# Two attention layers in one fused transformer kernel: row maxima split on VectorE and turned in 32x32 blocks instead of by TensorE

## The chip, the cores and the metric

The kernel runs on one NeuronCore of a Trainium2 chip. The metric is the device time of one launch, in microseconds (us). The engines are TensorE (PE; its weight loads are shown apart as PEld), VectorE (DVE), ScalarE (ACT), GpSimd (POOL) and SyncE (SP), which here issues most of the DMAs.

## The reference

Sixteen sequences of 256 tokens with 128 features pass through four blocks, each followed by a residual sum and a layer norm: a causal attention with 16 heads of 8 features (low-rank projections of queries and keys), a gated MLP 128-512-512-512-128, a second attention without a mask, and an expert MLP with top-1 routing.

```python
x = _layernorm(x + _L0_attn_ref(x, ...))   # causal, softmax(q k / sqrt(8)) v
x = _layernorm(x + _L0_ffn_ref(x, ...))    # silu gate, two 512x512 layers with gelu
x = _layernorm(x + _L1_attn_ref(x, ...))   # softmax(q k) / sqrt(128), then v
x = _layernorm(x + _L1_ffn_ref(x, ...))    # top-1 of 8 experts, each a rank-4 addition
```

## The kernel before, in words

The work is cut in 16 chunks, one sequence each, and four stages, `A0`, `F0`, `A1`, `F1` (attention, MLP, attention, expert MLP). Attention needs the scores twice. `pass1` computes them with queries on the partitions, from bf16 pieces of queries and keys (72 rows, `ROWS`), only to find the maximum of each query's row: VectorE reduces each PSUM bank into columns of `top`, [128 queries, 2 query blocks, head] (L799 for A1 and the first chunks of A0; for the other chunks of A0 a fused add and minimum, L788, since there the causal mask must be added). `pass2` computes the scores again with keys on the partitions. It must subtract the maximum of each query, and queries now run along the free dimension. So the negated maximum enters the product as three more rows of the queries' operand, bf16 pieces that add up to the fp32 value: 75 rows (`ROWSM`) at L1113. ACT takes the exponential (L643), and `values` (L1131) multiplies by v.

Getting the maxima from `top` into those three rows is the step `maxima`. It is done once per chunk and attention, except for chunk 0 of A0 (which adds the maxima in fp32 and stays as it is), and for the last chunk of A1 it is done in two halves (`early` for the first 8 heads). That makes 30 whole ones and 2 halves. Its parts before the change:

- PE waits until all maxima of the chunk are made, then transposes the two blocks of `top` with the identity into a shared PSUM bank (L1081; L1092 for the early half).
- DVE waits for that, and splits the 16x256 maxima from PSUM in three bf16 parts (cast, subtract, cast, subtract: L829, L831, L833, L835; L812 to L818 for the early half) into `tsplit`.
- SP waits for the parts and issues three DMAs of 8 KB, one for each row of `qrow` (L505; L513 for the early half).
- PE's `pass2` of this chunk waits for the DMAs (`trows`).

Each engine runs its steps in the order of a string, `SEQUENCE`, one letter for a step, written out for the whole kernel. The steps of several chunks are interleaved in it: while one chunk is in attention A0, an earlier one is in the MLP and a still earlier one in A1. An engine takes its letters strictly in turn, so a letter that waits holds all behind it. A second string, `BANK_TABLE`, gives each PE step its PSUM bank. The letters `warm` are multiplications of the identity (L988) with no use for the result.

## Time and profile before

| | |
|---|---|
| median of 3 runs | 895.47 us (893.18 to 896.65) |
| profiled execution, its own time | 896.33 us |
| its span in the trace | 894.6 us |
| PE busy | 867.6 us, 97% |
| PEld busy | 683.4 us, 76% |
| DVE busy | 700.9 us, 78% |
| ACT busy | 461.5 us, 52% |
| POOL busy | 195.8 us, 22% |
| TensorE's granted clock, mean | 0.984 |

The profiled execution has 1.7 us around its span and is 0.9 us above the median of the three runs. PE's busy time is a union of matmuls of which each is shown with its whole latency, so neighbours overlap, and 97% does not mean that PE works at its peak. The chain that ended last tells through which engine the end was reached.

### The profile page before, as it was taken

What the parts mean: (1) busy time and instruction counts of PE and PEld (TensorE: products, weight loads), DVE (VectorE), ACT (ScalarE), POOL (GpSimd) and SP (SyncE); (2) the same over time, 40 slices, a digit from 0 to 9 for tenths busy, and PEclk for the clock granted to TensorE, in tenths of its full rate; (3) what the DMA queues carried; (4) which work ended last, traced back from release to release, by engine and by line L of the source; (5) the groups of instructions that cost most, each with busy time, mean ns of one, the idle gap of its engine ahead of it and who ended that gap; (6) DMA issues with size and microseconds to landing.
All of it is one profiled execution on the core that took longest, in us unless ns stands there. A gap on an engine that the chain in (4) does not pass through costs nothing.

```text
span 894.6 us, 19356 instructions
## 1 busy us (share of the span) xinstructions
PE 867.6 (97%) x7132; PEld 683.4 (76%) x7132; DVE 700.9 (78%) x2490; ACT 461.5 (52%) x861; POOL 195.8 (22%) x395
## 2 busy tenths in 40 slices
PE   8989999999999999999999999999999999999997
PEld 6867687877667876688777887788866887878866
DVE  5667758778899769984998859996799859845874
ACT  2323454638456436665655736544466655582382
POOL 6332212003410133011500123012320314010211
PEclk9999799999899999999999999999999999999999
DMA  7324032321232034402142033210333022002200
GB/s 255 110 79 117 16 90 66 90 68 43 81 107 74 1 91 116 119 3 74 43 136 54 21 90 109 70 52 19 112 110 91 3 78 57 24 8 71 78 14 13
DMA packets 47982, 63.78 MB, mean 71 GB/s; under 512 B 5504, under 2 KB 41936, under 8 KB 43184
## 3 DMA queue, kind: packets, MB, share of 16 engines
q1 hardware_dynamic: 46208, 57.67, 22.7%
q10 hardware_dynamic: 1680, 4.87, 1.5%
q8 instruction: 57, 0.93, 0.4%
q14 instruction: 37, 0.30, 0.1%
HBM read 47.48 MB, written 14.29 MB: 69 GB/s over the span
## 4 chain that ended last, share of the span: by engine, by line
PE 74%; DVE 12%; DMA 5%; ACT 4%; issue 2%; SPq 2%; POOL 0%; ACTq 0%; POOLq 0%; DVEq 0%
PE banks L1182 23%; PE banks L1131 10%; PE banks L1113 8%; PE banks L1060 6%; PE banks L1164 6%; PE banks L1238 5%; DVE top L799 4%; DMA krow<-scratch 3%; PE banks L1001 2%; PE banks L1211 2%; PE banks L1051 1%; ACT prob L643 1%; PE banks L1143 1%; ACT L643 1%; PE banks L988 1%
## 5 line engine op out<-in xcount | busy, mean ns | idle before, releaser
L643 ACT ACTIVATE prob<-banks 128x384 f32<-128x384 f32 (+1 forms) x512 | 246.6, 552 | 102.8 <-PE banks L1113 57.6
L799 DVE TENSOR_REDUCE top<-banks 128x2 f32<-128x512 f32 (+1 forms) x268 | 166.9, 678 | 11.7 <-PE banks L1060 8.4
L1113 PE MATMUL banks<-qrow,krow 75*128 75x256 bf16 x992 | 148.7, 264 | 6.4 <-ACT prob L643 3.4
L788 DVE CUSTOM_DVE_ANT_0 banks<-banks,above 128x128 f32<-128x128 f32 x448 | 144.3, 386 | 11.8 <-PE banks L1060 7.6
L1060 PE MATMUL banks<-krow,qrow 72*128 72x256 bf16 x752 | 126.0, 276 | 3.7 <-ACT prob L643 1.9
L1131 PE MATMUL banks<-prob,v 128*32 128x256 f32 (+1 forms) x2048 | 121.2, 365 | 2.7 <-POOL prob L585 1.9
L1113 PEld LDWEIGHTS banks<-qrow,krow 75*128 75x128 bf16 x992 | 85.5, 99 | 43.7 <-ACT prob L643 13.6
L1182 PE MATMUL banks<-glu,wh 128*128 128x256 f32 x512 | 118.5, 385 | 0.2 <-DVE glu L900 0.2
L1182 PE MATMUL banks<-hid,wh 128*128 128x256 f32 x512 | 118.3, 385 | 0.0
L578 POOL TENSOR_TENSOR ln_rstd<-ln_var,minus_half 128x2 f32<-128x2 f32 x64 | 44.9, 705 | 300.1 <-DVE ln_var L879 299.7
L657 ACT ACTIVATE hid<-banks 128x512 f32<-128x512 f32 x64 | 38.1, 597 | 134.8 <-PE banks L1182 134.6
L1182 PEld LDWEIGHTS banks<-glu,wh 128*128 128x128 f32 x512 | 96.0, 192 | 13.9 <-DVE glu L900 0.6
L1182 PEld LDWEIGHTS banks<-hid,wh 128*128 128x128 f32 x512 | 96.1, 192 | 13.6 <-ACT prob L643 0.5
L1131 PEld LDWEIGHTS banks<-prob,v 128*32 128x32 f32 x2048 | 56.8, 111 | 50.0 <-issue 15.3
L1060 PEld LDWEIGHTS banks<-krow,qrow 72*128 72x128 bf16 x752 | 65.6, 99 | 27.5 <-ACT prob L643 5.7
L585 POOL TENSOR_SCALAR_AFFINE_SELECT prob<-prob 128x512 f32<-128x512 f32 x128 | 83.7, 654 | 0.0
L583 POOL TENSOR_TENSOR pool_carrier<-minus_half 128x1 f32<-128x1 f32 x128 | 28.4, 222 | 248.4 <-ACT prob L643 244.7
L573 POOL TENSOR_TENSOR resid<-x,rows 128x256 f32<-128x256 f32 x48 | 34.8, 726 | 143.9 <-DVE ln_sum L866 143.2
L1164 PE MATMUL banks<-xt,w 128*128 128x256 f32 x256 | 61.5, 387 | 0.3 <-ACT xt L648 0.2
L788 DVE DVE_READ_ACCUMULATOR2_ANT top<- 128x1 f32 x448 | 61.5, 137 | 0.0
L841 DVE STREAM_TRANSPOSE osum<-banks 128x256 f32<-128x256 f32 x64 | 28.2, 440 | 32.4 <-PE banks L1131 32.2
L1164 PEld LDWEIGHTS banks<-xt,w 128*128 128x128 f32 x256 | 46.9, 193 | 8.0 <-ACT xt L648 0.5
(125 smaller groups left out, 1181.2 us busy)
## 6 DMA issues: line engine op xcount, KB each, us to landing
qrow<-scratch SPq DMA_DIRECT2D x30, 576.0 KB
krow<-scratch SPq DMA_DIRECT2D x90, 192.0 KB
scratch<-split SPq DMA_DIRECT2D x93, 128.0 KB, 1.8
xt<-in_xt SPq DMA_DIRECT2D x16, 128.0 KB, 3.0
wh<-in_wh ACTq DMA_DIRECT2D x2, 1024.0 KB, 9.3
out<-xout SPq DMA_DIRECT2D x16, 128.0 KB, 2.2
x<-in_x SPq DMA_DIRECT2D x15, 128.0 KB, 3.6
qrow<-tsplit SPq DMA_DIRECT2D x90, 8.0 KB, 1.8
```

Of the source, the lines that this page charges most:

```text
L578: nc.gpsimd.tensor_tensor(ln_rstd[s][:], ln_var[s][:], minus_half[:], ALU.pow).then_inc(rstd[s], 1)
L585: nc.gpsimd.affine_select(out=diag, in_=diag, compare_op=ALU.is_ge, fill=0.0, base=0, pattern=[[0, 2], [0, QB], [1, P]], channel_multiplie ...
L643: nc.scalar.activation(prob[s][:, j % 2, g, 0:wide], banks[:, b, 0:wide], ACT.Exp, scale=1.0 / float(np.sqrt(np.float32(HD))) if s == A0 e ...
L657: nc.scalar.activation(hid[layer][:, 2 * m:2 * m + 2, :].rearrange("p m t -> p (m t)"), banks[:, g, :], ACT.Gelu).then_inc(gelued, 1)
L788: done = nc.vector.tensor_tensor_reduce(out=bank[:, g * wide:(g + 1) * wide], in0=bank[:, g * wide:(g + 1) * wide], in1=above[:, 2 * P - w ...
L799: nc.vector.tensor_reduce(out=dst, in_=src, axis=AX, op=ALU.max, negate=True).then_inc(maxed[s], 1)
L1060: done = nc.tensor.matmul(at, queries(h, qb), keys(h, 2), start=True, stop=not masked, skip_group_check=True)
L1113: done = nc.tensor.matmul(bank[:, kb * SEQ:(kb + 1) * SEQ - q0], krow[s][n % DEEP[s]][0:ROWSM, h, kb * P:(kb + 1) * P], qrow[s][n % DEEP[s ...
L1131: done = nc.tensor.matmul(banks[32 * i:32 * i + 32, g, q0:SEQ], v[s][:, kb, GROUP * j + i, :], prob[s][:, j % 2, i, kb * SEQ:(kb + 1) * SE ...
L1164: done = nc.tensor.matmul(banks[:, g, i * TOK:(i + 1) * TOK], w12[:, side, (2 * m + i) * P:(2 * m + i + 1) * P], xt[F0][n % AHEAD][:], sta ...
L1182: done = nc.tensor.matmul(banks[:, g, i * TOK:(i + 1) * TOK], wh[:, layer, k, (2 * m + i) * P:(2 * m + i + 1) * P], (glu, hid[0])[layer][: ...
L1238: done = nc.tensor.matmul(banks[:, g, t * D:(t + 1) * D], src[:, k, t * P:(t + 1) * P], w[:, k, :], start=k == 0, stop=k == HB - 1)
```

## The change

The maxima are no longer turned by PE. `top` shrinks to [128, 32], column 2h + q for head h and query block q. VectorE splits it in three bf16 parts as it lies, [128, 3, 32] (`tpart`), and then turns it with four transposes of 32 partitions by 3 x 32 elements, which land in `tsplit`, [32 (head, block), 3, 128]. SP's three DMAs per chunk now read 32 rows of 128 elements in place of 16 rows of 256, the same bytes. PE has no step for it, and no PSUM bank is used. The step is called `tops` (`half_tops` for the early half, which computes and turns all 32 columns, and of which SP takes 16 rows). Both fall on DVE and SP only. Chunk 0 of A0 keeps PE's transposes. Two memsets of `top` on POOL are gone.

```diff
-        top = {s: sb(f"top{s}", [P, QB, P]) for s in (A0, A1)}
-        tsplit = {s: sb(f"tsplit{s}", [32 + HALF, PARTS, SEQ], BF16) for s in (A0, A1)}
-        trest = {s: sb(f"trest{s}", [32 + HALF, SEQ]) for s in (A0, A1)}
+        top = {s: sb(f"top{s}", [P, HEADS * QB]) for s in (A0, A1)}
+        tpart = {s: sb(f"tpart{s}", [P, PARTS, HEADS * QB], BF16) for s in (A0, A1)}
+        tsplit = {s: sb(f"tsplit{s}", [32, PARTS, P], BF16) for s in (A0, A1)}
+        trest = {s: sb(f"trest{s}", [P, HEADS * QB]) for s in (A0, A1)}
...
+            def spread_tops(s, n, heads, there):
                 for i in range(PARTS):
+                    sp.dma_start(qrow[s][n % DEEP[s]][ROWS + i:ROWS + i + 1, heads, :].rearrange("o h (q t) -> o (h q) t", q=QB),
+                                 tsplit[s][heads.start * QB:heads.stop * QB, i, :]).then_inc(there, DMA)
...
-                    sp.dma_start(qrow[s][n % DEEP[s]][ROWS + i:ROWS + i + 1, there, :],
-                                 tsplit[s][0:HALF if n == HALVED[s] else HEADS, i, :]).then_inc(trows[s], DMA)
...
+            def parts_of_tops(s, done, k):
+                t, r = tpart[s], trest[s][:]
+                nc.vector.tensor_copy(t[:, 0, :], top[s][:]).then_inc(done, 1)
+                dve.wait_ge(done, k + 1)
+                nc.vector.tensor_tensor(r, top[s][:], t[:, 0, :], ALU.subtract).then_inc(done, 1)
+                dve.wait_ge(done, k + 2)
+                nc.vector.tensor_copy(t[:, 1, :], r).then_inc(done, 1)
+                dve.wait_ge(done, k + 3)
+                nc.vector.tensor_tensor(t[:, 2, :], r, t[:, 1, :], ALU.subtract).then_inc(done, 1)
+                dve.wait_ge(done, k + 4)
+                for b in range(P // 32):
+                    turned = nc.vector.transpose(tsplit[s][:, :, bass.ts(b, 32)], t[bass.ts(b, 32)])
+                turned.then_inc(done, 1)
+
+            def tops(s, n):
+                k = rowed_before(s, n)
+                dve.wait_ge(maxed[s], S1[s] * n + S1[s])
...
+                    dve.wait_ge(trows[s], NTOPS * k)
+                parts_of_tops(s, tparts[s], 5 * k)
...
             def maxima(s, n, g):
-                dve.wait_ge(top_full[s], 1 * n + 1)
...
-                nc.vector.tensor_copy(t[:, 0, :], src).then_inc(tparts[s], 1)
...
             def maxima(s, n, g):
-                pe.wait_ge(maxed[s], S1[s] * n + S1[s])
...
-                for qb in range(QB):
-                    done = nc.tensor.transpose(banks[:, g, qb * P:(qb + 1) * P], top[s][:, qb, :], ident[:])
-                done.then_inc(top_full[s], 1)
-                last.used(g, tparts[s], 4 * rowed_before(s, n) + 2)
```

The strings `SEQUENCE` of all five engines and `BANK_TABLE` are new. The number of every other kind of step is the same, the 34 `warm` steps among them; their order differs in many places by a few steps. Two places show the kind.

On PE, the end of the scores of chunk 3 of A0 (`maxima`), which is the third of the 32. L1060 is `pass1`, L1113 `pass2`, L1131 `values`, L1182 a layer of the MLP, L1238 its last layer. Before:

```order
L1060 MATMUL banks<-krow_1,qrow_1 128x256 x2
L1113 MATMUL banks<-qrow_0,krow_0 128x256
L1113 MATMUL banks<-qrow_0,krow_0 128x128
L1182 MATMUL banks<-hid,wh 128x256 x8
L1081 MATMUL banks<-ident,top 128x128 x2
L1131 MATMUL banks<-prob,v 32x256 x4
L1131 MATMUL banks<-prob,v 32x128 x4
L1131 MATMUL banks<-prob,v 32x256 x4
L1131 MATMUL banks<-prob,v 32x128 x4
L1238 MATMUL banks<-w,hid 128x128 x8
```

and with the change (L1059 is `pass1`, L1169 the layer, L1118 `values`, L1225 the last layer):

```order
L1059 MATMUL banks<-krow_1,qrow_1 128x256 x2
L1169 MATMUL banks<-hid,wh 128x256 x8
L1059 MATMUL banks<-krow_1,qrow_1 128x256 x2
L1118 MATMUL banks<-prob,v 32x256 x4
L1118 MATMUL banks<-prob,v 32x128 x4
L1118 MATMUL banks<-prob,v 32x256 x4
L1118 MATMUL banks<-prob,v 32x128 x4
L1225 MATMUL banks<-w,hid 128x128 x8
```

The transposes are gone, and the last step of `pass1` now stands behind the layer instead of ahead of it.

On DVE, the end of the last chunk of A1. L799 reduces a bank of scores, L866 to L879 are the sum and the statistics of a layer norm, and L829 to L835 split the last 8 heads' maxima. Before:

```order
L799 TENSOR_REDUCE top<-banks 128x2 x3
L866 TENSOR_TENSOR ln_sum<-banks,resid 128x256
L871 BN_STATS ln_parts<-ln_sum 128x6 x2
L874 MEMSET dve_carrier 128x1
L876 BN_AGGR ln_stat<-ln_parts 128x2 x2
L879 TENSOR_SCALAR ln_var<-ln_stat 128x2
L829 CAST tsplit<-banks 16x256
L831 TENSOR_TENSOR trest<-banks,tsplit 16x256
L833 CAST tsplit<-trest 16x256
L835 TENSOR_TENSOR tsplit<-trest,tsplit 16x256
```

and with the change (L794 reduces, L806 to L815 are the new step, L865 on is the layer norm):

```order
L794 TENSOR_REDUCE top<-banks 128x2 x3
L806 CAST tpart<-top 128x32
L808 TENSOR_TENSOR trest<-top,tpart 128x32
L810 CAST tpart<-trest 128x32
L812 TENSOR_TENSOR tpart<-trest,tpart 128x32
L815 STREAM_TRANSPOSE tsplit<-tpart 32x3x32 x4
L865 TENSOR_TENSOR ln_sum<-banks,resid 128x256
L870 BN_STATS ln_parts<-ln_sum 128x6 x2
L873 MEMSET dve_carrier 128x1
```

The step now follows the last reduction directly, where the layer norm's sum and statistics stood between.

## Rows read from the trace of the kernel before

**Rows 1.** Page, part 4: the chain that ended last, by engine.

```profile
PE 74%; DVE 12%; DMA 5%; ACT 4%; issue 2%; SPq 2%; POOL 0%; ACTq 0%; POOLq 0%; DVEq 0%
```

**Rows 2.** Windows of 50 us: PE, PEld, DVE, ACT, POOL busy (instructions), granted clock, DMA.

```profile
250.00:300.00 50.00, 48.11 (x410) 35.51 (x409) 47.56 (x204) 30.70 (x55) 4.95 (x8) 1.00 0.26 71
350.00:400.00 50.00, 49.72 (x427) 37.65 (x427) 47.12 (x200) 32.01 (x56) 2.92 (x6) 1.00 0.26 73
400.00:450.00 50.00, 49.09 (x408) 39.60 (x408) 34.58 (x105) 28.65 (x53) 17.86 (x38) 1.00 0.22 62
450.00:500.00 50.00, 48.35 (x380) 37.69 (x379) 45.16 (x167) 29.85 (x52) 4.17 (x6) 0.97 0.31 83
550.00:600.00 50.00, 49.81 (x456) 37.40 (x455) 47.20 (x187) 26.40 (x51) 6.50 (x10) 1.00 0.27 79
650.00:700.00 50.00, 48.84 (x454) 34.99 (x455) 48.20 (x184) 27.17 (x55) 5.50 (x11) 1.00 0.30 85
```

**Rows 3.** Groups by line and form: the first split step and the transposes.

```profile
L829 DVE CAST tsplit<-banks 16x256 bf16<-16x256 f32 x31 | 12.4, 401 | 16.0 <-PE banks L1081 15.8
L1081 PE MATMUL banks<-ident,top 128*128 128x128 f32 x62 | 12.4, 281 | 0.0
L1081 PEld LDWEIGHTS banks<-ident,top 128*128 128x128 f32 x62 | 7.4, 143 | 3.2 <-issue 1.4 <-DVE top L799 0.9
```

**Rows 4.** The chain in order of time: first and last of 22 pieces of L1081, and L1092.

```profile
55.60 0.45 PE banks L1081 x2
...
855.11 0.37 PE banks L1092 x2
...
860.56 0.27 PE banks L1081 x2
```

**Rows 5.** Timeline of DVE, 111 to 118 us, and of PE there.

```profile
113.91 0.41 DVE L829 CAST tsplit<-banks 16x256 bf16<-16x256 f32 x1 [4.78 <-PE banks L1081]
115.11 0.41 DVE L835 TENSOR_TENSOR tsplit<-trest,tsplit 16x256 bf16<-16x256 f32 x1
...
108.33 5.32 PE L1182 MATMUL banks<-hid,wh 128*128 128x256 f32 x16
113.49 0.38 PE L1081 MATMUL banks<-ident,top 128*128 128x128 f32 x2
```

**Rows 6.** Timeline of DVE, 218 to 223 us: small steps, overlapping writes, a transpose.

```profile
218.27 0.18 DVE L914 TENSOR_TENSOR pick<-logit,best 128x16 f32<-128x16 f32 x1
218.48 0.18 DVE L915 TENSOR_TENSOR pick<-pick,ranks 128x16 f32<-128x16 f32 x1
...
221.42 0.45 DVE L855 STREAM_TRANSPOSE yt<-osum 128x256 f32<-128x256 f32 x1
221.79 0.58 DVE L773 TENSOR_TENSOR v<-banks,rows 128x64 f32<-128x64 f32 x4
```

**Rows 7.** The chain in order of time, 221 to 231 us: wait for the rows.

```profile
224.52 0.56 SPq L505
...
225.12 0.59 SPq L505
...
225.75 3.81 DMA qrow<-tsplit
```

**Rows 8.** Timeline near the end, DVE: the last chunk's maxima.

```profile
858.38 1.95 DVE L799 TENSOR_REDUCE top<-banks 128x2 f32<-128x512 f32 x3 [0.16 <-PE banks L1060]
...
861.71 0.41 DVE L829 CAST tsplit<-banks 16x256 bf16<-16x256 f32 x1
```

**Rows 9.** Page, part 6: a row's DMA, KB each, median us to landing.

```profile
qrow<-tsplit SPq DMA_DIRECT2D x90, 8.0 KB, 1.8
```

**Rows 10.** Timeline: first and last of eleven L829 in the five busy windows of DVE.

```profile
265.42 0.41 DVE L829 CAST tsplit<-banks 16x256 bf16<-16x256 f32 x1
...
692.32 0.37 DVE L829 CAST tsplit<-banks 16x256 bf16<-16x256 f32 x1
```

**Rows 11.** A window of 10 us, columns as in the 50 us windows: the clock.

```profile
100.00:110.00 10.00, 9.94 (x70) 6.12 (x71) 5.75 (x35) 6.88 (x15) 6.18 (x16) 0.57 0.01 2
```

More of the change, by code:

```diff
@@ L140 @@
+        "zMlTzMGGTzMTzMGKGTTTTT"
     ),
@@ L184, in sequence @@
         n, i = divmod(seen[letter], len(parts_of(name, stage)))
-        if name == "early":
+        if name in ("early", "half_tops"):
             n = EARLY[stage]
         seen[letter] += 1
-        if stage == A0 and (name in ("qk", "fetch") or name == "maxima" and engine == "sp"):
+        if stage == A0 and name in ("qk", "fetch", "tops"):
             n += 1
@@ L432, in build @@
         S2 = HEADS
+        NTOPS = PARTS * DMA
         NWEIGHTS1 = 4 * DMA
@@ L536, in _ @@
             nc.gpsimd.memset(hid[1][:].rearrange("p m t -> p (m t)"), 0.0).then_inc(wex_cleared, 1)
-            nc.gpsimd.memset(top[A0][:].rearrange("p q h -> p (q h)"), 0.0)
             nc.gpsimd.memset(minus_half[:], -0.5)
@@ L779, in pass1 @@
                 bank = banks[:, b, :]
-                h, to = GROUP * j, top[s]
-                if n == HALVED[s]:
-                    h, to = (32 + h, top_early[s]) if j < HALVES else (h - HALF, top[s])
+                h, to = GROUP * j, top[s][:].rearrange("p (h q) -> p q h", q=QB)
+                if u == 0:
+                    if j == 0 and rowed_before(s, n) > 0:
+                        dve.wait_ge(tparts[s], 5 * rowed_before(s, n) - 3)
+                    elif j == HALVES and n == HALVED[s]:
+                        dve.wait_ge(early_parts[s], 2)
                 if s == A0 and n >= BY_PE:
@@ L924, in route @@
                 done.then_inc(routed, 1)
-            walk(dict(scale=scale, qk=split_, v=v_, pass1=pass1, maxima=maxima, early=early, osum=bring, outputs=outputs, project=project, down=sum_,
+            walk(dict(scale=scale, qk=split_, v=v_, pass1=pass1, maxima=maxima, tops=tops, half_tops=half_tops, early=early, osum=bring, outputs=outputs, project=project, down=sum_,
                       norm=norm, gated=gate, route=route), "dve")
@@ L1074, in maxima @@
             def maxima(s, n, g):
-                pe.wait_ge(maxed[s], S1[s] * n + S1[s])
+                pe.wait_ge(maxed[s], S1[s])
                 last.wait(pe, g)
-                if s == A0 and is_first(n):
-                    turn_tops(1, g).then_inc(top_full[s], 1)
-                    return
-                for qb in range(QB):
-                    done = nc.tensor.transpose(banks[:, g, qb * P:(qb + 1) * P], top[s][:, qb, :], ident[:])
-                done.then_inc(top_full[s], 1)
-                last.used(g, tparts[s], 4 * rowed_before(s, n) + 2)
+                turn_tops(1, g).then_inc(top_full, 1)
             def early(s, n, g):
-                pe.wait_ge(maxed[s], S1[s] * n + S1[s] // 2)
+                pe.wait_ge(maxed[s], S1[s] // 2)
                 last.wait(pe, g)
-                if s == A0:
-                    turn_tops(0, g).then_inc(early_full[s], 1)
-                    return
-                for qb in range(QB):
-                    done = nc.tensor.transpose(banks[:, g, qb * P:(qb + 1) * P], top_early[s][:, qb, :], ident[:])
-                done.then_inc(early_full[s], 1)
-                last.used(g, early_parts[s], 2)
+                turn_tops(0, g).then_inc(early_full, 1)
             def pass2(s, n, j, g, b):
                 if j == 0 and g == 0 and n == HALVED[s]:
-                    pe.wait_ge(early_rows[s], PARTS * DMA)
+                    pe.wait_ge(early_rows[s], NTOPS)
                 if s == A0 and is_first(n):
@@ L1102, in pass2 @@
                 elif j == (HALVES if n == HALVED[s] else 0) and g == 0:
-                    pe.wait_ge(trows[s], PARTS * DMA * rowed_before(s, n) + PARTS * DMA)
+                    pe.wait_ge(trows[s], NTOPS * rowed_before(s, n) + NTOPS)
                 h = GROUP * j + g
```

183 lines of the change are left out of this document (78 added, 105 removed).

## The prediction

> **What bounds the kernel now.** I read the page's chain first. It says through whom the end was reached: PE has 74% of it, DVE 12% [rows 1]. Then the windows of 50 us, since a mean over the run hides that the limits alternate. In five of them DVE is busy 45.2 to 48.2 of 50 us and PE's weight loads only 35 to 38; in others, such as 400 to 450 us, DVE is at 34.6 and the loads at 39.6 [rows 2]. PE's matmul busy time is near 50 everywhere, and that tells little: neighbours overlap. So the kernel is bound by PE in most places, with DVE close behind or level with it in about 250 us. Both matter here, since the change takes work from PE and leaves its counterpart on DVE.
>
> The Trainium skill, "Perfetto Trace Analysis", section "Identifying the Most-Contended Engine", says the same of matmul busy time: it is no measure of how full TensorE is, and the busy share of weight loads is a better one. By it PE (76%) and DVE (78%) are level and a saving on PE alone should bring less than the chain's share; the chain, at 74% on PE, speaks for more. What that rule would make of the time is the second rival below.
>
> **What goes from PE.** 31 pairs of L1081 and one of L1092, 64 transposes [rows 3]. A matmul's mean of 281 ns is its latency. What a pair holds of PE is seen in the chain: 0.22 us where PE runs on, 0.27 to 0.45 where it came out of a wait [rows 4]. 32 x 0.22 = 7.0 us of PE's work. Of that the chain itself passes through 22 pieces of L1081, which I added to 6.1 us, and through L1092 with 0.4: 6.5 us on the path, which I take off.
>
> The weight loads ahead of the transposes show 3.2 us of idle time, 0.9 for the last maximum on DVE and 1.4 as issue behind such a wait [rows 3]. PE now never waits for `top` outside of chunk 0; the next such wait is for the DMA'd rows, which existed before too. I take off 2.3 us.
>
> **What stays on DVE.** Before, the four steps run from 113.91 to 115.52, 1.6 us [rows 5]; each is a 16x256 operation, so its time is mostly 256 elements. Now they are 128x32. No row has these shapes; the nearest are the router's dependent 128x16 steps, which start 0.21 us apart [rows 6]. With 16 more elements at about 1 ns, 0.22 each, 0.9 for four.
>
> Then the four transposes, each of 96 elements on 32 partitions. The nearest row is the transpose of 256 elements, 0.45 us [rows 6]; with 160 elements fewer at 1 ns each, an estimate of 0.28. One behind the other that makes 1.1 us. If they overlap as the four 128x64 writes of L773 do, 0.58 for four, 0.145 each [rows 6], with 32 more elements each at 1 ns, it is 0.7. If each also has a gap of 0.04 before it, 1.3. So the step costs DVE 1.6 (as now) to 2.2 us. I take them one behind the other, since the row of the same operation counts for more than one of another whose writes all lie in the same partitions: 2.0 us, or 0.4 more than now. 32 x 0.4 = 13 us more of DVE work in all, 0 to 19 by the two ends.
>
> The Trainium skill, "VectorE: DVE Perf Modes", section "Two Vector instructions with no wait between them", speaks against the overlap: an instruction whose first input starts in another quarter of the partitions than the last one's is held until all earlier ones are done. The four transposes read from four different quarters. No row here has such a succession. With the rule the step costs 2.0 us or more, and the sum below stands; without it the step is 1.6 and the sum is 4.4 us less.
>
> What of it is on the path: eleven of the 32 steps lie in the five windows in which DVE is nearly full [rows 10, 2]. There 11 x 0.4 = 4.4 us are added. Elsewhere DVE has 5 us or more free in 50 and PE's MLP layers stand beside it, so there the price is nothing; if that cover were gone, it would be the other 21 x 0.4 = 8.4.
>
> **The hand-over.** DVE no longer waits for PE's transposes: 15.8 us over ten times [rows 3]. The longest, 4.78 us, stood at 109 to 114 us because the transposes were queued behind a whole MLP layer on PE (5.3 us) [rows 5]. PE was working all that time, so the end is not moved by it; what stood behind the wait on DVE (a transposition of `osum`, v) was not late for PE. I count nothing. In the new order PE runs the layer ahead of the last `pass1` there.
>
> Near the end there is a gain. The last reduction ends at 858.38 + 1.95 = 860.33, the split starts at 861.71, since the transposes and a layer norm's statistics stood between [rows 8]. Now the step follows at once. 1.4 earlier less 0.4 for its own length: 1.0 us, and PE has little left to hide it with. I take off 1.0.
>
> SP issues the same 96 DMAs, 0.6 us each in a row [rows 7], of pieces half as long. They took 1.8 us to land [rows 9]; in one place the chain waited 3.81 [rows 7]. No row shows 256-byte pieces; I take no change, with 0 as the least and, at a guess from the 1.8 to 3.8 above, up to 1 us more in each of the three places where such a landing is in the chain. The two memsets less on POOL run beside the first loads: nothing.
>
> **The new order.** The letters are the same in number but for the 30 + 1 taken from PE. I compared the PE work that stands between a chunk's last `pass1` and its first `pass2`. It is mostly 1 to 3 us shorter than before. So the new order relies on the rows' coming sooner, which the hand-over allows (at least the 0.4 us of a pair and its start, up to the 4.8 of a queue behind it), but on a step whose length on DVE nobody has measured. If the step were 1 us longer than I think, PE would stand in places where it did not. I take no gain or loss of its own.
>
> **The sum.** 896.3 (own time of the profiled execution) - 6.5 - 2.3 + 4.4 - 1.0 = 890.9. The profiled execution is 0.9 above the median of the runs, so 890.0.
>
> **Rivals.**
> 1. DVE becomes the bound, slower. The mechanism: the four transposes, one by one, with their start-up, and every step of DVE behind them late, where PE and ACT wait for banks to be reduced. For it speaks that DVE is at 94% and more in four windows. Price at the upper end: 32 x 0.6 = 19 us against the 9.8 saved: 895.5 + 9 = 904.7 if all of it were on the path; with the eleven and half of the others, 21.5 x 0.6 - 9.8 = 3.1, 898.6. It decides from about 0.3 us more per step if all 32 are exposed (9.8 / 32), or 0.9 us more if only the eleven are.
> 2. No change: PE's saving goes into waits. Where DVE is the limit, the 7 us less of PE work only lets PE wait longer. The chain runs through PE even there, but as one path among several of equal length. Eleven of 32 pairs stand there; with the 4.4 us on DVE this gives 895.5 - 6.5 x 21/32 + 4.4 - 1.0 = 894.6, between 892 and 898.
> 3. More gain. The transposes overlap (-4.4) and the DVE waits of 15.8 us were partly on the path through the order, a third of them: 890.0 - 4.4 - 5.3 = 880.3. For it speaks that all engines' orders were made anew with one dependency between PE and DVE less; against it that PE was rarely idle at those waits.
> 4. The step doesn't do what it says. The DMAs need all four transposes, and no PE work is left in it, so I see no way for that.
>
> The clock adds noise to any of them: in the window of 100 to 110 us it was granted at 0.57, so mostly at the lower level of 1.2 GHz, while PE was shown busy [rows 11]. Over the run 1.6% of the clock was missing, 14 us' worth; a few us more or less of it move the result by as much.
>
> **How the numbers follow.** Forecast as summed, 886 to 894: 0.46. No change, 892 to 898: 0.19. DVE bound, 898 to 905: 0.18. More gain, below 886: 0.17. The likeliest is 890. A range of 881 to 900 leaves out about half of "more gain" and most of what DVE would cost, 0.2 in all. A measurement of this kernel tells 0.5%, 4.5 us, from no change: faster means below 891.0, slower above 900.0. Faster: somewhat under two thirds of the forecast and all of "more gain", 0.29 + 0.17 = 0.46. Slower: nearly all of DVE bound, 0.16. Same: the rest, 0.38.
>
> **What the profile after would show.** L1081's successor absent but for chunk 0's; PE 64 matmuls fewer. The four small steps together at 0.9 us and the transposes 0.25 to 0.3 each, and 0.7 or 1.1 for four by their start times: that settles the overlap. DVE busy near 701 + 13 = 714 us if not overlapped. DVE's wait for PE at the split gone. At the end, the split right behind the last reduction. The five windows: if DVE is at 49 there and they are longer, rival 1 is at work; if PE waits there for DVE's `top` more than before, rival 2. The prediction is wrong if a step takes over 2.3 us on DVE, if the rows' DMA takes more than 2.8 us to land, or if the new order has put a wait on PE that this reading does not see.

## The result and the profile after

| | before | changed |
|---|---|---|
| median of the runs | 895.01 us | 903.35 us (901.53 to 911.61) |
| ratio | 1 | 1.0088, 95% interval 1.0053 to 1.0124 |
| profiled execution, its span | 896.33, 894.6 us | 901.53, 899.7 us |
| mean granted clock | 0.984 | 0.978 |

The kernel became 8 us slower, 0.9%; 890 was forecast, 13 us lower. Here and below, ratios and intervals leave out the executions over 1.5% longer than the fastest of the same kernel (one or two in each of seven kernels, one of them of 2171 us, and one of 1887 us of the kernel before), and the medians keep them. The page of the changed kernel, parts 1 and 4:

```profile
PE 865.4 (96%) x7068; PEld 678.2 (75%) x7068; DVE 717.6 (80%) x2618; ACT 450.6 (50%) x853; POOL 194.3 (22%) x393
...
PE 58%; DVE 21%; DMA 8%; issue 5%; ACT 4%; SPq 3%; POOL 1%; POOLq 0%; DVEq 0%; ACTq 0%
```

PE has 64 matmuls fewer, as it should. DVE went from 700.9 to 717.6 us. The chain left PE (74% in [rows 1]): DVE's share grew from 12 to 21%, the DMAs' from 5 to 8%. Of the chain's DMAs the rows of this step are 12.7 us in five places, for 9.5 in three before; those that fetch the keys (`krow<-scratch`) went from 23 to 37 us. The keys' part can't be put down to the length of the step: before_one_part below, with a short step, has 40 us. The step itself, on the timeline of DVE and then of SyncE's queue:

```profile
243.07 0.14 DVE L806 CAST tpart<-top 128x32 bf16<-128x32 f32 x1
243.24 0.19 DVE L808 TENSOR_TENSOR trest<-top,tpart 128x32 f32<-128x32 f32 x1
243.47 0.18 DVE L810 CAST tpart<-trest 128x32 bf16<-128x32 f32 x1
243.68 0.19 DVE L812 TENSOR_TENSOR tpart<-trest,tpart 128x32 bf16<-128x32 f32 x1
243.91 1.11 DVE L815 STREAM_TRANSPOSE tsplit<-tpart 32x96 bf16<-32x96 bf16 x4
...
245.05 1.83 SPq L499 DMA_DIRECT2D qrow<-tsplit  x3
```

From 243.07 to 245.02 it takes 1.95 us, where the old one took 1.6 [rows 5]; four transpositions in 1.11 us are one behind the other. The chain in order of time over the same place shows what hangs on it:

```profile
243.68 0.20 DVE tpart L812
...
244.75 0.28 DVE tsplit L815
...
245.05 0.56 SPq L499
...
246.29 2.59 DMA qrow<-tsplit
...
248.93 0.41 PE banks L1100 x2
```

PE's first matmul on the rows starts 3.9 us behind the end of the last transposition: two issues of the queue, then the last copy's issue and landing. By this chain every tenth of a us on DVE is a tenth for PE here. PE waits 1.06 us, and the windows of 5 us around it (busy time of PE, PEld, DVE, ACT and POOL, then the granted clock and the DMAs' share) show a second price:

```profile
240.00:245.00 5.00, 5.00 (x42) 3.49 (x46) 4.75 (x15) 1.12 (x3) 0.78 (x2) 1.00 0.61 174
245.00:250.00 5.00, 3.77 (x40) 2.61 (x38) 4.90 (x13) 2.15 (x5) 0.00 (x0) 0.99 0.34 93
250.00:255.00 5.00, 4.93 (x30) 2.88 (x34) 4.78 (x19) 3.77 (x8) 1.64 (x3) 0.50 0.50 136
255.00:260.00 5.00, 5.00 (x54) 2.64 (x50) 1.77 (x4) 2.87 (x6) 0.44 (x1) 0.83 0.58 152
```

The granted clock falls to its lower level, 1.2 GHz, behind the gap. By the view of waits, PE's matmuls waited twice for these rows before, 0.7 us in all, and three times for `x`, a layer norm's output from DVE, 0.9 us in all. Now (us in total, times, the longest):

```profile
PE banks L1100 <- DMA qrow<-tsplit: 4.1, 6, 1.1
PE banks L1139 <- DVE x L888: 3.0, 6, 0.7
```

So the waits for the rows themselves grew by 3.4 us. PE's idle time, span less busy time, grew from 27 to 34 us.

### The profile page after: what moved, and what is told of

The parts are those of the page before. It is cut to its first block, busy times and chain, and to the rows that moved or that the text cites. A ratio compares the mean times of both kernels' runs of the same rounds, so it can differ in the third digit from the quotient of the medians.

```text
span 899.7 us, 19347 instructions
## 1 busy us (share of the span) xinstructions
PE 865.4 (96%) x7068; PEld 678.2 (75%) x7068; DVE 717.6 (80%) x2618; ACT 450.6 (50%) x853; POOL 194.3 (22%) x393
## 4 chain that ended last, share of the span: by engine, by line
PE 58%; DVE 21%; DMA 8%; issue 5%; ACT 4%; SPq 3%; POOL 1%; POOLq 0%; DVEq 0%; ACTq 0%
PE banks L1169 19%; PE banks L1118 7%; PE banks L1100 7%; DVE top L794 7%; PE banks L1059 5%; DMA krow<-scratch 4%; PE banks L1225 4%; PE banks L1151 3%; ACT prob L634 2%; DVE x L888 2%; PE banks L1000 2%; PE banks L1198 2%; DMA scratch<-split 2%; DVE tsplit L815 1%; DMA qrow<-tsplit 1%
## 5 line engine op out<-in xcount | busy, mean ns | idle before, releaser
L794 DVE TENSOR_REDUCE top<-banks 128x2 f32<-128x512 f32 (+1 forms) x268 | 167.0, 678 | 16.3 <-PE banks L1059 12.7
L1100 PE MATMUL banks<-qrow,krow 75*128 75x256 bf16 x992 | 152.2, 269 | 8.3 <-DMA qrow<-tsplit 4.1
L1059 PE MATMUL banks<-krow,qrow 72*128 72x256 bf16 x752 | 126.6, 276 | 5.5 <-DMA krow<-scratch 1.9
L1118 PE MATMUL banks<-prob,v 128*32 128x256 f32 (+1 forms) x2048 | 121.2, 367 | 0.7 <-DVE top L794 0.2
L1169 PE MATMUL banks<-hid,wh 128*128 128x256 f32 x512 | 119.7, 389 | 0.0
L1169 PE MATMUL banks<-glu,wh 128*128 128x256 f32 x512 | 116.6, 381 | 1.2 <-DVE glu L895 1.2
L1169 PEld LDWEIGHTS banks<-hid,wh 128*128 128x128 f32 x512 | 97.6, 195 | 13.5 <-ACT hid L648 0.2
L1169 PEld LDWEIGHTS banks<-glu,wh 128*128 128x128 f32 x512 | 94.8, 190 | 14.6 <-DVE glu L895 1.4
L1118 PEld LDWEIGHTS banks<-prob,v 128*32 128x32 f32 x2048 | 58.0, 111 | 47.6 <-issue 16.6
L1059 PEld LDWEIGHTS banks<-krow,qrow 72*128 72x128 bf16 x752 | 66.0, 99 | 30.6 <-issue 4.5
```

What stands on the lines that cost most here:

```text
L794: nc.vector.tensor_reduce(out=dst, in_=src, axis=AX, op=ALU.max, negate=True).then_inc(maxed[s], 1)
L1059: done = nc.tensor.matmul(at, queries(h, qb), keys(h, 2), start=True, stop=not masked, skip_group_check=True)
L1100: done = nc.tensor.matmul(bank[:, kb * SEQ:(kb + 1) * SEQ - q0], krow[s][n % DEEP[s]][0:ROWSM, h, kb * P:(kb + 1) * P], qrow[s][n % DEEP[s ...
L1118: done = nc.tensor.matmul(banks[32 * i:32 * i + 32, g, q0:SEQ], v[s][:, kb, GROUP * j + i, :], prob[s][:, j % 2, i, kb * SEQ:(kb + 1) * SE ...
L1169: done = nc.tensor.matmul(banks[:, g, i * TOK:(i + 1) * TOK], wh[:, layer, k, (2 * m + i) * P:(2 * m + i + 1) * P], (glu, hid[0])[layer][: ...
```

## The experiments

Each ran in five rounds beside the kernel before (896 us each time), so they are compared by their ratios to it; 0.001 is 0.9 us. Two ratios whose intervals are 0.003 to each side differ clearly from about 0.004, 4 us, on. "PE's pairs" are the 32 pairs of transpositions of the maxima; "idle" are pairs of the identity in their places. "Step" is the length of one step on DVE, read from the timelines or worked out from the rows of its operations.

| kernel | order | PE's pairs | step, us | DVE busy | ratio (95% interval) |
|---|---|---|---|---|---|
| before_one_part | old | yes | 0.4 | 666.9 | 0.9969 (0.9944 to 0.9993) |
| before | old | yes | 1.6 | 700.9 | 1 |
| before_pe_pairs_twice | old | twice | 1.6 | 700.7 | 1.0062 (1.0036 to 1.0088) |
| before_split_once_more | old | yes | 2.0 | 712.6 | 1.0066 (1.0039 to 1.0093) |
| before_split_longer | old | yes | 2.5 | 727.7 | 1.0276 (1.0232 to 1.0321) |
| old_order_one_turn | old | no | 1.1 | 685.0 | 0.9913 (0.9883 to 0.9944) |
| three_turns_put_back | old | no | 1.7 | 705.1 | 0.9985 (0.9963 to 1.0008) |
| old_order_three_turns | old | no | 1.7 | 703.6 | 1.0033 (1.0010 to 1.0057) |
| old_order_new_step | old | no | 2.0 | 711.5 | 1.0090 (1.0056 to 1.0125) |
| half_step_put_back | old | no | 2.0 | 711.4 | 1.0082 (1.0055 to 1.0110) |
| new_step_pe_pairs_kept | old | idle | 2.0 | 711.9 | 1.0092 (1.0054 to 1.0130) |
| pe_pairs_kept_put_back | old | idle | 2.0 | 711.7 | 1.0086 (1.0054 to 1.0119) |
| old_order_one_part_turned | old | no | 1.0 | 684.0 | 0.9940 (0.9919 to 0.9961) |
| new_order_one_turn | new | no | 1.1 | 694.0 | 0.9873 (0.9838 to 0.9907) |
| new_order_three_turns | new | no | 1.7 | 709.8 | 0.9983 (0.9945 to 1.0021) |
| changed kernel | new | no | 2.0 | 717.6 | 1.0088 (1.0053 to 1.0124) |
| new_order_filled_waits | new | no | 2.0 | 717.1 | 1.0021 (0.9995 to 1.0048) |
| new_order_turned_at_once | new | no | 1.1 | 697.3 | 1.1875 (1.1825 to 1.1926) |
| new_order_one_part | new | no | 1.0 | 692.6 | 0.9833 (0.9800 to 0.9865) |
| new_order_one_part_at_once | new | no | 0.4 | 673.4 | 0.9875 (0.9823 to 0.9926) |

### Step or order?

**old_order_new_step.** The new step in the old tables: PE's row without its 32 entries, DVE's and SyncE's entries renamed, the half step of the last chunk 5 places earlier. The first row of PE's table:

```diff
-        "abcbdcbbbcccbbcebbcbbffbffffgffhffhffffbbbfbbbbcbcbbbfbhchadicfffffffffjfffhffffhshhsaditbbbbbbbjtbbbsbb"
+        "bbbbcbbadebbffbbfccbbffgfffffhfhffffhfbbbbccbbcbbbbbcbhccaccidffffffffffffjhfffhfshhasidbbbbbtbjbtbbbbbs"
```

> The changed step on DVE (split, four transposes), but all engines in the order of the kernel before, with PE's transposes of the maxima simply taken out of it; only the early half on DVE moved up five places. Theory O (the new order is too tight: it starts pass2 1 to 3 us of PE work sooner, the rows are not there, PE stands and its clock drops after it): the step alone costs little and saves PE's 7 us, so 888 to 893 us, clock 0.98 or more, PE's idle time before pass2 for the rows as in the kernel before. Theory S (the step itself costs, since DVE is level with PE): 899 to 904, as the changed kernel.

902.63 us, 1.0090, against 1.0088 with the new order: the step makes the loss without the new order, and between the orders there is no difference to be told (4.5 us either way). The two get there differently. The mean granted clock over the executions was 0.982 in the old order and 0.974 in the new one (0.987 for the kernel before), so the new order loses more by the clock and, as it seems, is ahead by something else; `new_order_filled_waits` bears on that.

**new_order_one_turn** and **old_order_one_turn.** Three of the four transpositions are left out, in the new and in the old order; 96 of each 128 queries keep a constant of -8 per part in place of their maxima.

```diff
-                for b in range(P // 32):
-                    turned = nc.vector.transpose(tsplit[s][:, :, bass.ts(b, 32)], t[bass.ts(b, 32)])
-                turned.then_inc(done, 1)
+                nc.vector.transpose(tsplit[s][:, :, 0:32], t[0:32]).then_inc(done, 1)
```

> The changed kernel with one of the four transposes of a step; the other three blocks of 32 queries keep a constant in place of their maxima, so the output is wrong for them. DVE gets 32 x 0.8 = 26 us less, and the rows are ready 0.8 us sooner. Theory O: the waits of 1.1 to 1.3 us for the rows shrink to 0.3 to 0.5, the clock stays up, 893 to 898. Theory S: all of the price of the step is DVE time, which falls by 26 us, 885 to 892.

> The order of before with the new step, and one of the four transposes (three blocks of queries keep a constant, output wrong there). Against the same order with four it shows the price of 0.8 us of DVE per step without the new order. Theory O: 1 to 4 us less than with four (only the eleven steps in the full windows count). Theory S: 8 us or more less.

887.03 and 890.99 us: 19 and 16 us less than with four turns, for 26 us of transpositions, as theory S had it. DVE's time decides. Whether it is its load or the 0.8 us by which each row comes sooner, these two can't tell, since both shrink. The new order is 3.6 us ahead of the old here, within the noise of the pair (4 us). The expectations call the output wrong; but the constant is one shift for all scores of a query, like the maximum, and leaves the softmax what it is as long as the exponentials stay in range.

**new_order_filled_waits.** The changed kernel with a few matmuls of the identity ahead of three stages at which PE waited and the clock fell (248, 286 and 371 us; four, seven and four calls, each two matmuls in the trace).

```diff
+            def fill(kind, s, n, b):
+                last.wait(pe, b)
+                for _ in range(FILL.get((kind, s, n), 0)):
+                    nc.tensor.matmul(banks[:, b, 0:P], ident[:], ident[:], start=True, stop=True)
```

> The changed kernel, with useless 128x128 matmuls put ahead of three of PE's longest waits (4 before pass2 of chunk 2 and of chunk 5 of A1, 7 before pass1 of chunk 7 of A0, 0.22 us each), so that PE is busy while it waits. Nothing else changes. Theory C (the drops of the clock after those waits make up the loss): the drops at 250, 290 and 375 us are gone, some 10 us of half speed, clock 0.985 and 897 to 900 us. If only the waits themselves count: the drops may go, but the time stays within 1 us of 903.

899.46 us, 1.0021: 6 us less than the changed kernel, give or take 4. Theory C is borne out. Its windows of the same place keep the clock:

```profile
245.00:250.00 5.00, 4.87 (x45) 3.11 (x45) 4.76 (x17) 1.57 (x4) 0.00 (x0) 1.00 0.28 85
250.00:255.00 5.00, 4.64 (x45) 3.34 (x47) 4.89 (x15) 3.49 (x7) 0.52 (x1) 1.00 0.52 148
```

PE was given more to do, useless as it is, and the kernel got faster. So part of the loss is the clock behind the waits, not the waits. But one of the three waits, the longest of all that PE's matmuls have in the changed kernel, was not for the step's rows. It was for the keys of the next chunk. The chain in order of time, from the end of a step (264.23 to 266.22 us on DVE) on:

```profile
265.95 0.27 DVE tsplit L815
...
271.67 0.44 DVE split L751
272.11 0.02 issue
272.13 0.70 DVE split L753
272.83 0.02 issue
272.85 3.71 DMA scratch<-split
...
278.89 7.60 DMA krow<-scratch
286.49 0.05 issue
286.54 0.40 PE banks L1050 x4
```

PE stood still for 1.66 us ahead of 286.54. So a step reaches PE by two ways here: by its rows, and by what stands behind it on DVE, here the split of keys. Before, PE's longest wait for keys was 1.2 us, and the clock stood at 1.00 from 280 to 300 us, where now it was 0.74 and 0.91 in the windows from 285 and from 290 us. How much of the loss goes the second way was not measured; no run fills that wait alone.

### What is PE's saving worth?

**new_step_pe_pairs_kept.** PE keeps 32 pairs of transpositions of the identity.

```diff
+            def load_alone(g):
+                last.wait(pe, g)
+                for qb in range(QB):
+                    nc.tensor.transpose(banks[:, g, qb * P:(qb + 1) * P], ident[:], ident[:])
```

> The old order with the whole step on DVE (old_order_new_step, 902.6 us), but PE keeps a pair of 128x128 transpositions at each of the 32 old places, of the identity matrix instead of the maxima, into the bank that the old step took: it waits for no maximum, only for its bank. PE's load alone is put back (about 7 us), DVE's stays as in the new step. What PE computes here goes nowhere; the output is the same. Theory E (the 7 us taken from PE were worth next to nothing, since DVE decides): 900 to 905 us, within 2 us of old_order_new_step. Theory P (PE's saving was real, as the prediction had it, and the new step costs even more on DVE): 908 to 912 us.

1.0092 against 1.0090 without them: theory E, PE's load alone is worth next to nothing. The pairs can also have kept the clock up a little: its mean was 0.985 with them and 0.982 without, at most 2 of the 7 us.

**before_pe_pairs_twice.**

```diff
-                for qb in range(QB):
-                    done = nc.tensor.transpose(banks[:, g, qb * P:(qb + 1) * P], top[s][:, qb, :], ident[:])
+                for _ in range(2):
+                    for qb in range(QB):
+                        done = nc.tensor.transpose(banks[:, g, qb * P:(qb + 1) * P], top[s][:, qb, :], ident[:])
```

> The kernel before, with each of PE's 32 pairs of transpositions of the maxima done twice: 64 more matmuls, 7 us more of PE at full clock, and about 0.2 us more between a maximum and DVE's split of it. Theory P (PE's time counts for the share of the chain that it has, about three quarters, as the prediction had it): 901 to 903 us, 5 to 7 us more than before. Theory E (DVE and the path of the maxima decide together with PE, so that PE alone is worth little): 895 to 899 us.

901.95 us, 1.0062: 5.6 us more, as theory P had it. Added work on PE costs here; but it also puts 0.2 us between each maximum and its split, and the run doesn't tell the two apart.

**before_split_longer** and **before_split_once_more.** The last operation of the split three times or twice.

```diff
                 nc.vector.tensor_tensor(t[:, 2, :], r, t[:, 1, :], ALU.subtract).then_inc(tparts[s], 1)
+                for i in (4, 5):
+                    dve.wait_ge(tparts[s], 6 * k + i)
+                    nc.vector.tensor_tensor(t[:, 2, :], r, t[:, 1, :], ALU.subtract).then_inc(tparts[s], 1)
```

> The kernel before, with the last operation of the split done three times instead of once in each of the 32 steps: 64 more operations of DVE of about 0.2 us, 13 to 14 us of DVE in all, 0.4 us more in each step, which makes the step as long as the new one (2.0 us) while PE keeps its transpositions and the old order stays. Theory E (each us of DVE is worth the 0.45 us by which the one-turn kernels went down): 895.5 + 6 = 900 to 904 us. Theory P (only the steps that PE waits for count, 11 of 32 by the prediction): 4.4 us more at most, 896 to 900 us. Should it reach 903, the length of the step is all there is to the loss.

> The kernel before, with the last operation of the split done twice in each of the 32 steps: 0.43 us more of DVE in each (14 us in all), so that the step is 2.0 us long like the new one; PE, its transpositions and the old order as before. It is the middle point between before (1.6 us, 896) and before_split_longer (2.5 us, 921). If length alone makes the loss and the loss grows faster than the length: 901 to 905 us, the same as the new step in the old order, so that PE's saving has nothing in it. If the loss is a straight line: 908 to 910, and then PE's saving is worth 6 us after all, lost in a longer step.

I had mis-sized the first: an added operation takes 0.43 us, not 0.2 (group of before_split_longer):

```profile
L841 DVE TENSOR_TENSOR tsplit<-trest,tsplit 16x256 bf16<-16x256 f32 x62 | 26.9, 434 | 2.1
...
PE 57%; DVE 27%; DMA 6%; issue 4%; ACT 3%; SPq 2%; POOL 0%; ACTq 0%; DVEq 0%; POOLq 0%
```

The first 0.43 us per step (DVE busy 11.7 us more) cost 5.9 us, the second (15.1 us more) 19, give or take 5. The price bends: what is below the slack of an order costs less, what is above it is paid in full or more. The chain of before_split_longer reads like that of the changed kernel, with PE's transpositions in place.

**before_one_part.** One bf16 part of the maximum in place of three: the shift is the same for all scores of a query, so it need not be exact.

```diff
-ROWSM = ROWS + PARTS
+TPARTS = 1
+ROWSM = ROWS + TPARTS
```

> The kernel before, with the maxima kept in one bf16 part in place of three: the same shift is taken from all scores of a query and its weights are divided by their sum, so the shift need not be the exact maximum. It leaves out three of the step's four DVE operations (96 of 128, about 20 us of DVE), two of three copies to rows, and two of the 75 contraction rows of the scores' matmuls; PE's transpositions stay. Theory E: 0.45 us for each us of DVE off, 885 to 888 us, and a little more for the shorter step from the maximum to its rows (1.6 to about 0.4 us): 880 to 888. Theory P (DVE counts only where PE waits for it, 5 steps of the chain): 889 to 893 us.

893.75 us, 0.9969: 34 us less of DVE, and a step of 0.4 us for 1.6, bring 2.8. The bend again, from its flat side; theory P came close (893 at the upper end), theory E had far more. DVE alone doesn't bound this kernel.

**old_order_three_turns.** As the one-turn kernel, with three.

> The old order with the step on DVE, but three of the four transpositions: the last 32 queries of each block of 128 keep a constant of -8 per part in place of their maxima. DVE's load is then that of before within 2 to 3 us (711.5 less 8.5, against 700.9), the step is about 1.7 us long (1.6 before, 2.0 with four), and PE has no transposition of maxima left: PE's saving alone. Theory P (it is worth the share of the chain): 887 to 890 us. Theory E (next to nothing while the step on DVE is as long as before): 895 to 899 us. By the one-turn kernel (891.0 for 26 us less DVE than with four turns, 902.6) a straight line gives 898.7; if the loss grows faster than the step's length, as before_split_longer says, 893 to 896.

899.36 us, 1.0033, a little above all the figures. Its windows show a loss of its own, where the moved half step stands ahead of a reduction for which PE waits:

```profile
845.00:850.00 5.00, 3.60 (x29) 2.13 (x31) 4.69 (x13) 4.59 (x8) 0.00 (x0) 0.89 0.01 3
850.00:855.00 5.00, 5.00 (x38) 2.74 (x41) 2.14 (x5) 1.42 (x3) 0.00 (x0) 0.50 0.10 29
```

**half_step_put_back**, **three_turns_put_back**, **pe_pairs_kept_put_back** have the half step in its old place, where it splits only its own 16 columns:

```diff
-                nc.vector.tensor_copy(t[:, 0, :], top[s][:]).then_inc(done, 1)
+                nc.vector.tensor_copy(t[:, 0, c], top[s][:, c]).then_inc(done, 1)
```

> old_order_new_step (902.6 us, 1.009 of before) with DVE's half step of the last chunk back in its old place, behind the five operations that it had been put ahead of; it splits only the 16 columns of its own half, so that the reductions of the other half need not wait for it. If the move made the loss at 850 us in every run, not only in the profiled one: 898.5 to 900 us, and no clock under 0.9 between 845 and 865 us. If it did not: 902 to 903 us.

> old_order_three_turns (899.4 us, 1.0033) with the half step put back in the same way: PE without its transpositions, DVE with the load of before (704 against 701 us), the old order everywhere; the last 32 queries of each block of 128 keep a constant of -8 per part. Theory P (PE's saving was real and the moved step ate it): 891 to 894 us, faster than before. Theory E (PE's 7 us are worth next to nothing at the old load of DVE): 895 to 898 us.

> half_step_put_back with a pair of transpositions of the identity kept on PE at each of the 32 old places (they wait for no maximum, only for their bank). Against half_step_put_back it is PE's 7 us alone, with DVE's step 2.0 us long in both. Theory P: 5 to 7 us more than half_step_put_back, so 904 to 906. Theory E: within 2 us of it, 899 to 901.

903.46, 895.29 and 902.52 us. The first says that with four turns the move of the half step had cost nothing that can be told (1.0090 to 1.0082); the others agree with theory E, the last by its distance to half_step_put_back (its 899 to 901 rested on a lower figure for that kernel). With three turns the move had cost 4.3 us, give or take 3 (1.0033 to 0.9985), so it is not a fixed price in every kernel. In the trace of half_step_put_back a gap of PE stands at 860 us too, but the clock doesn't fall behind it:

```profile
860.00:865.00 5.00, 4.12 (x46) 2.54 (x48) 4.23 (x13) 4.79 (x10) 0.00 (x0) 1.00 0.05 16
865.00:870.00 5.00, 4.97 (x57) 3.57 (x50) 4.77 (x16) 3.64 (x7) 0.00 (x0) 1.00 0.05 12
```

PE's 7 us are worth 1.0086 less 1.0082, and 1.0092 less 1.0090 in the pair above: 0.3 us by both, each within 4 to 5. With PE free of its pairs and DVE nearly at its load of before, three_turns_put_back, the gain is 1.3 us (3.3 less to 0.7 more). DVE is 4.2 us above its old load there, which at the price of the first 0.43 us (5.9 us for 11.7) is 2 us; by that estimate PE's saving may be worth 3 us at the old load, still less than half of what was taken off.

**new_order_three_turns.**

> The changed kernel with three of the four transpositions (the last 32 queries of each block of 128 keep a constant of -8 per part): 8.5 us less DVE than the changed kernel, 0.28 us less in each step. Between the changed kernel (1.0088 of before) and new_order_one_turn (0.9873). If the loss bends as in the old order, where the last turn alone cost a whole us for each us of DVE: 893 to 896 us. If it is a straight line between the two: 896 to 898.

896.84 us, 0.9983. The median lies in the range of the straight line, the ratio times 896 (894.5) in that of the bend, so it decides nothing. The fourth turn costs 9.4 us in the new order for 7.8 of DVE, the two before it 9.9 for 15.8; in the old order 5.1 or 8.7 against 10.8 or 6.5 (half step moved or not at three turns). In the new order, and in the old one with the half step in its place, the last turn costs more than each of the two before it; with the half step moved it does not (5.1 against 5.4). None is sharp enough to prove a bend; the before_split pair shows it.

### How the rows get there, and a version that beats both

**new_order_turned_at_once.** One transposition over 128 partitions, each block in its own quarter, and twelve copies in place of three.

```diff
-                for b in range(P // 32):
-                    turned = nc.vector.transpose(tsplit[s][:, :, bass.ts(b, 32)], t[bass.ts(b, 32)])
-                turned.then_inc(done, 1)
+                nc.vector.transpose(tsplit[s][:].rearrange("p i t -> p (i t)"), t[:].rearrange("p i t -> p (i t)")).then_inc(done, 1)
...
+                    for b in range(P // 32):
+                        sp.dma_start(row[:, b], tsplit[s][32 * b + heads.start * QB:32 * b + heads.stop * QB, i, :]).then_inc(there, DMA)
```

> The changed kernel, with the four transpositions of a step made one: a single instruction over all 128 partitions turns each block of 32x32 in its own quarter of the partitions, and the rows are then fetched by twelve small copies (one for each part and each quarter, 64 bytes a row) instead of three. Exact maxima, the new order. DVE loses 96 instructions, 26 us, as in new_order_one_turn (887.0 us), the step is about 1.2 us long; SyncE issues nine copies more in each step. If the copies land in about the same 1.9 us: 886 to 890 us, faster than before. If their issue and landing cost half a us more in each step: 890 to 895. If they cost a us or more: 897 or above.

1064.35 us, far from all three figures. The queue, and PE's group:

```profile
458.85 7.75 SPq L501 DMA_DIRECT2D qrow<-tsplit  x12
...
L1099 PE MATMUL banks<-qrow,krow 75*128 75x256 bf16 x992 | 183.4, 314 | 112.5 <-DMA qrow<-tsplit 112.4
```

A copy holds SyncE's queue for 0.6 us, at 2 KB as at 8 KB (twelve 7.75, three 1.83 us), and the rows count as there with their last copy. Nine more are 5.5 to 5.9 us in each of 32 steps, 176 to 189 us; the kernel is 177 us above new_order_one_turn. That looks like payment in full, but two things make it up: PE's matmuls waited 112 us for the rows, and the granted clock was 0.886 where new_order_one_turn had 0.981. The order has nothing like that slack.

**new_order_one_part** has one part in place of three in the changed kernel (three of the small operations and two of the copies fewer; 1.3 us less on the queue):

```diff
-                dve.wait_ge(done, k + 1)
-                nc.vector.tensor_tensor(r, top[s][:], t[:, 0, :], ALU.subtract).then_inc(done, 1)
...
-                    turned = nc.vector.transpose(tsplit[s][:, :, bass.ts(b, 32)], t[bass.ts(b, 32)])
+                    turned = nc.vector.transpose(tsplit[s][:, 0, bass.ts(b, 32)], t[bass.ts(b, 32), 0, :])
```

> The changed kernel with the maxima kept in one bf16 part in place of three (the same shift for all scores of a query, so the softmax stays what it is): three small operations of four and two copies of three fall away in each step, 73 contraction rows for 75. The four transpositions of a third of the width stay. If a transposition's time is mostly fixed (about 0.2 us for a third of the width), DVE loses about 26 us, the step is about 1.0 us: 886 to 890 us. If the order made for the long step binds from there on, no lower than new_order_one_turn, 887.

882.05 us, 0.9833: 15 us under before and 21 to 23 under the changed kernel, lower than I had expected and the fastest of all. It takes load off DVE, shortens the step and shortens the way of the rows at once. Its group of transpositions and part 4 of its page:

```profile
L810 DVE STREAM_TRANSPOSE tsplit<-tpart 32x32 bf16<-32x32 bf16 x128 | 25.6, 200 | 2.4
...
PE 79%; DVE 8%; ACT 5%; issue 3%; DMA 3%; POOL 1%; SPq 1%; POOLq 0%; DVEq 0%; ACTq 0%
```

**old_order_one_part_turned** is the same step in the old order.

> new_order_one_part's step (one bf16 part, one cast, four transpositions of a third of the width, one copy for the rows) in the old order, with the half step in its old place. If the new order is worth what the one-turn kernels showed (887.0 new, 891.0 old): 885 to 887 us. If the two orders are level for a short step: 881 to 883.

890.12 us, 0.9940, above both figures. The new order is worth 9.6 us with this step, give or take 3 (3.6 with one turn, give or take 4), and nothing that can be told with the step that it came with. Which part of it does this was not tested. One difference stands in every trace: ACT loads its tables 63 times in the new order and 71 times in the old, at 1.28 us each, 10 us less for an engine that is half busy.

**new_order_one_part_at_once**: one transposition for four, four copies for one.

> new_order_one_part (882.05 us) with its four transpositions made one over all 128 partitions, and the row fetched by four copies in place of one. DVE loses 96 instructions of 0.2 us, 19 us, and 0.6 us of each step; SyncE issues three copies more at about 0.6 us each, 1.8 us more between DVE's end and the rows, so that the way from the last maximum to its rows grows by 1.2 us while DVE's load falls. If DVE's load decides: 875 to 882 us. If the way decides, at the price that new_order_turned_at_once paid for its nine copies (1064.35 less 887.03, 177 us for 5.5 us a step, 32 steps): 882 + 32 x 1.2 = 920 at most; with the slack that a shorter step has, 888 to 910.

887.73 us, 0.9875: 3.8 us more than new_order_one_part, with intervals that overlap, and by four executions (two more, of 896 and 901 us, are not in the ratio). DVE's 19 us less gave no gain beside 1.2 us more on the way of the rows. By this pair the load of DVE alone is not what the short step gains by.

## Why the prediction was wrong

- **What bounds the kernel** was read half right. DVE level with PE in five windows was seen; the chain's 74% was then taken as a price list. It is one path, and says nothing of how far the next one is behind.
- **"What goes from PE", 6.5 and 2.3 us: the step that failed.** It took 8.8 us off for work that left PE's part of the chain. With the new step's length that work is worth 0.3 us (within 4 to 5 in each of two pairs of kernels), near the old load of DVE 1.3 us (-0.7 to 3.3), or 3 by the estimate above. 8.5 of the 13 us between forecast and measurement lie here. Rival 2 had said this and got 0.19. The Trainium skill, "Perfetto Trace Analysis", section "Identifying the Most-Contended Engine", which puts the load share above matmul time, had the two engines level at 76 and 78%. The runs agree for a saving on PE alone (0.3 us of 7). An addition did cost (before_pe_pairs_twice, 5.6 us for 7, with a longer path in it). A reading that fits, not one that is shown: of two level engines either costs if it grows, and neither pays much if it shrinks alone (PE's pairs 0.3 us, DVE's 34 us 2.8), while both together do (old_order_one_turn, 7.8 us).
- **"What stays on DVE"** was right in its size: 1.95 us for 2.0, transpositions of 0.267 us for 0.28, four in 1.11 for 1.1, 0.84 for 0.9 from the first small operation to the transpositions. DVE busy, 717.6 for 714, is in part luck: the step's own operations add 9.2 us (50.5 to 59.7), and the other 7.5 are other operations that ran longer in the new order, the layer norm's `x` 36.5 us for 33.3 among them. In the old order the step made it 711.5. The four came one behind the other, as "VectorE: DVE Perf Modes" of the Trainium skill, section "Two Vector instructions with no wait between them", has it for inputs in different quarters.
- **"What of it is on the path", 4.4 us**, was a term mis-sized. The same 0.4 us per step costs 5.9 us beside PE's pairs (before_split_once_more) and 7.3 to 8.2 as the new step (the other kernels with a step of 2.0 us and no filled waits), with intervals that overlap. Counting the eleven steps in full windows took a step as either hidden or not; the chain of the changed kernel runs through 14 steps, and the clock falls behind some of the waits.
- **The hand-over, 1.0 us at the end**: the split now starts right behind the last reduction (865.93 for 865.89 us), as put. No time of a kernel shows what it is worth. The rows' copies land in 1.9 us in the median, for 1.8.
- **The new order**, "no gain or loss of its own": so in the changed kernel, but it seems by luck, as a sum of two things: it is ahead by something that shows with a step of 1.0 us (9.6 us), and it has waits behind which the clock falls. The warning beside it, that it relies on a step whose length nobody had measured, was the better sentence. The sign of being wrong, a wait on PE that the reading does not see, came: 1.66 us for keys at 286 us.
- **The clock**, "a few us more or less", was taken as noise, and in the new order it is a price: filling three waits gave 6 us back (about 2 to 10) of the 8. In the old order the clock was higher (0.982 to 0.985 for 0.974) and the loss the same, so there more of it is something else.
- The sum with the measured terms: 895.0 + 7.7 to 8.2 for the step (the two kernels that keep PE's load, in the old order) - 0.3 for PE = 902.4 to 902.9; measured 903.35. Rival 1, 898 to 905, has the time, and its mechanism, every step of DVE behind the transpositions late, is seen at 264 to 286 us. Its sum is right by luck: it has 0.6 us more per step against 9.8 us saved, where the step was 0.4 us longer and nothing was saved. The sign that it named, DVE at 49 of 50 us in the five windows, did not come (42.0, 44.3, 47.6, 47.9 and 48.0, the first two with the clock at 0.90), so DVE was not filled to the end.

What stays open: what the half step's place costs, which differs between two kernels; whether the step costs by what it delays on DVE or by the time at which its rows come; what the new order gains with a short step; and how much of the bend is the clock and how much the queueing behind a late step, since no kernel held the clock at one level throughout.

## What to carry to other kernels

Where two engines are level, don't price a saving by its engine's share of the chain: ask what the same work costs on the engine that it goes to, since taking it from one of two level engines may bring nothing (0.3 us of 7 here). An order written out for one length of a step has a slack; test the length first (one operation twice, or left out), because the price bends there, here from 0.1 us per us of DVE to about 1.2. And look at what the step is for: an exact maximum in three parts was not needed. Leaving two of them out took 21 to 23 us from the changed kernel, though only 2.8 from the kernel before, whose DVE and PE were not relieved together.

## What the runs showed that I had not expected

- A transposition of a 32x32 block of bf16 takes 200 ns, of three such blocks 267 ns, and one over 128 partitions, the work of four, 278 ns: width is cheap and count is dear.
- A copy of the rows held SyncE's queue for 0.55 to 0.59 us in the median, at 2 KB as at 8 KB, and now and then for up to 1.6; twelve of 2 KB took 7.75 us.
- A wait of PE of about 1 us was followed by 5 us at a granted clock of 0.50 (250 to 255 us); with eight matmuls of the identity in its place the clock stayed at 1.00 there. The waits of 0.7 and 0.2 us that PE has at 860 us in half_step_put_back had no such fall behind them.
